# Second experts of an audio tower: the last 64 rows of the first product on half the array, slots in pairs

## What is computed

```
def _L1_ffn_ref(x, router_w, w1, w2):          # x = layernorm(h)
    logits = xt @ router_w.T ; probs = softmax(logits)
    topk_w, topk_idx = top_k(probs, 8) ; topk_w = topk_w / sum(topk_w)
    comb = zeros.at[token, topk_idx].add(topk_w)
    for e in range(16):
        h = gelu(xt @ w1[:, off:off + wd])
        out = out + comb[:, e:e + 1] * (h @ w2[off:off + wd, :])
```

## Time and profile before

| | before |
|---|---|
| three runs, median (lowest to highest) | 2683.68 us (2673.09 to 2688.26) |
| profiled execution, its own time | 2670.19 us |
| its span | 2668.2 us, mean granted clock 0.859 |
| TensorE busy (PE) over the span | 88% |
| VectorE, ScalarE, POOL busy | 68%, 58%, 3% |
| loads of d_1 and d_2 (3072 KB, 2304 KB), issue to landing | 11.6 and 16.6 us |

### The profile page before, as it was taken

The page is one execution under the profiler, slowest core; times in us unless marked ns, Lnnn a source line. Parts: engine busy times, 40 slices in busy tenths (PEclk is TensorE's granted clock), DMA queues, the critical chain, the costliest instruction groups (busy, mean ns, idle before and its releaser), DMA issues.

```text
span 2668.2 us, 40522 instructions
## 1 busy us (share of the span) xinstructions
PE 2355.6 (88%) x11650; PEld 2007.8 (75%) x11650; DVE 1826.5 (68%) x6297; ACT 1534.5 (58%) x4873; POOL 72.9 (3%) x46
## 2 busy tenths in 40 slices
PE   6778888999889998898988989878886999999999
PEld 2457667777768777777877877767775999899998
DVE  4278888989889898988989878887541322222223
ACT  2599887878768787776777766642111222222222
POOL 0000000000000000000000000000000101110110
PEclk7655587889889898888888879789986999999999
DMA  2000021222212221212222212223330000000000
GB/s 69 1 1 1 1 66 53 61 55 60 51 47 58 54 59 50 56 53 52 57 52 56 53 45 59 53 59 83 96 124 1 4 7 3 6 6 6 3 6 10
DMA packets 166682, 109.25 MB, mean 41 GB/s; under 512 B 15222, under 2 KB 165724, under 8 KB 166108
## 3 DMA queue, kind: packets, MB, share of 16 engines
q1 hardware_dynamic: 163872, 103.49, 14.5%
q10 hardware_dynamic: 2592, 3.33, 0.4%
HBM read 103.31 MB, written 3.20 MB: 40 GB/s over the span
## 4 chain that ended last, share of the span: by engine, by line
PE 44%; DVE 37%; issue 8%; ACT 6%; POOL 2%; another core or an unknown queue 1%; DVEq 1%; DMA 1%; SPq 0%; ACTq 0%; POOLq 0%
PE bank L503 20%; PE bank L848 7%; DVE late L1433 4%; DVE late L1295 3%; PE bank L617 3%; DVE late L1410 3%; DVE late L1407 3%; ACT late L972 3%; DVE late L1413 2%; DVE late L1403 2%; DVE late L1557 2%; PE bank L680 2%; POOL arena L485 2%; PE bank L582 2%; PE bank L738 2%
## 5 line engine op out<-in xcount | busy, mean ns | idle before, releaser
L972 ACT ACTIVATE late<-arena,late 125x250 bf16<-125x250 f32 x1152 | 565.0, 498 | 1.4 <-DVE late L1281 1.3
L1665 DVE TENSOR_TENSOR pair<-pair,arena 128x500 f32<-128x500 f32 x192 | 139.3, 726 | 444.8 <-PE bank L848 345.0
L503 PE MATMUL bank<-extra,wgu 128*128 128x250 f32 x1536 | 439.1, 437 | 0.0
L503 PE MATMUL bank<-xT,late 128*128 128x250 f32 x1536 | 360.6, 377 | 0.0
L503 PEld LDWEIGHTS bank<-extra,wgu 128*128 128x128 f32 x1536 | 326.7, 222 | 43.0 <-issue 2.2
L1138 ACT ACTIVATE pair<-bank 128x500 f32<-128x500 f32 x192 | 112.7, 587 | 382.9 <-PE bank L503 382.7
L503 PEld LDWEIGHTS bank<-xT,late 128*128 128x128 f32 x1536 | 286.5, 192 | 26.2
L617 PEld LDWEIGHTS bank<-vaug,late 125*125 125x125 f32 x1536 | 241.5, 233 | 76.0 <-ACT late L983 39.9
L848 PE MATMUL bank<-late,pair 128*125 128x192 f32 x1536 | 281.4, 326 | 0.0
L582 PE MATMUL bank<-late 16*125 16x251 f32 x768 | 251.8, 453 | 17.4 <-ACT arena L949 16.4
L848 PEld LDWEIGHTS bank<-late,pair 128*125 128x125 f32 x1536 | 259.3, 188 | 9.5 <-DVE pair L1665 0.2
(11 more groups left out here) (188 smaller groups left out, 3707.0 us busy)
## 6 DMA issues: line engine op xcount, KB each, us to landing
wgu<-in_b_g SPq DMA_DIRECT2D x192, 128.0 KB, 2.5
wgu<-in_b_u SPq DMA_DIRECT2D x192, 128.0 KB, 2.7
wdn<-in_b_d SPq DMA_DIRECT2D x192, 96.0 KB, 1.9
late<-comb_rows SPq DMA_DIRECT2D x128, 125.0 KB, 3.0
late<-comb_rows SPq DMA_DIRECT2D x128, 62.5 KB, 2.6
late<-in_d SPq DMA_DIRECT2D x1, 3072.0 KB, 11.6
out_h<-extra ACTq DMA_DIRECT2D x16, 187.5 KB
late<-in_d SPq DMA_DIRECT2D x1, 2304.0 KB, 16.6
```

The costliest lines, as they stand in the source:

```text
L503: ins = pe.matmul(dst, lhs(t), rhs(t), start=t == 0, stop=t == 1)
L972: ins = sc.activation(mk[:, n_par(u), t, :] if k == 3 else junk[:, t, :], s_sb[:, ub, t, 0:N], ACT.Sign, bias=thr[:, (n_par(u) + k + 1) % ...
L1665: dv.tensor_tensor(hid[:, s % 2, :, :], gl[:, s % 2, :, :], c, ALU.mult).then_inc(hid_set[1], 1)
```

## The change

In words: the product of channels 128 to 191 has 64 rows. The tiles are taken in pairs of slots (2j and 2j + 1). Slot 2j's 64-row weights lie on partitions 0 to 63, slot 2j + 1's on 64 to 127, and the products of the two slots go by turns to the lower and the upper half of the array: lower, upper, lower, upper. For the upper half the 64 channels must also lie on partitions 64 to 127 of `xT`, so VectorE writes them a second time into columns 192 to 255 of `xn`. The order on TensorE becomes first products 2j and 2j + 1, second products 2j - 2 and 2j - 1; the preparation of the next batch stands after pairs 0, 1 and 3. The first product's banks are four instead of three. The order on ScalarE, VectorE and POOL is the old one. The weights are loaded in three transfers.

```diff
         n_loads["c"] += 48
+        n_loads["d"] += 32
+        def m1_bank(s):
+            return bank[(1, 2, 3, 7)[s % 4]]
...
-                    sp.dma_start(w[name][:], d[name]).then_inc(loaded[k], 16)
+                    if name == "d_1":
+                        dst, of = w["d_1"], d["d_1"]
+                        sp.dma_start(dst[:, 0, :], of[:, 0, :]).then_inc(loaded[k], 16)
+                        for lo in (0, 1):
+                            half = dst[64 * lo:64 * lo + 64, 1, :].rearrange("p (t x n) -> p t x n", x=2, n=256)
+                            sp.dma_start(half[:, :, lo, :], of[0:64, 1, :].rearrange(
+                                "p (t x n) -> p t x n", x=2, n=256)[:, :, lo, :]).then_inc(loaded[k], 16)
+                    else:
+                        sp.dma_start(w[name][:], d[name]).then_inc(loaded[k], 16)
...
-            def m1_up(b, p, s):
-                ge(pe, gelu_set, 12 * b + s - 2)
-                for i in (0, 1):
-                    at = 128 * (2 * s + i)
-                    ins = two_k(bank[1 + s % 3][:, i * N:(i + 1) * N],
-                                lambda t: w["d_1"][:, t, at:at + 128], lambda t: xT[:, p, t, :])
-                ins.then_inc(up_ps[1], 1)
+            def m1_up(b, p, j):
+                ge(pe, gelu_set, 12 * b + 2 * j - 2)
+                X, Y = (m1_bank(2 * j + x) for x in (0, 1))
+
+                def product(U, x, i, k):
+                    tile = 4 * j + 2 * x + i
+                    lo = 0 if k == 0 else 64 * x
+                    hi = 128 if k == 0 else lo + 64
+                    return pe.matmul(U[:, i * N:(i + 1) * N], w["d_1"][lo:hi, k, 128 * tile:128 * tile + 128],
+                                     xT[lo:hi, p, k, :], start=k == 0 and i == 0, stop=k == 1,
+                                     skip_group_check=True)
+
+                for U, x in ((X, 0), (Y, 1)):
+                    for i in (0, 1):
+                        product(U, x, i, 0)
+                product(X, 0, 0, 1)
+                product(Y, 1, 0, 1)
+                product(X, 0, 1, 1).then_inc(up_ps[1], 1)
+                product(Y, 1, 1, 1).then_inc(up_ps[1], 1)
...
-                    for s in range(12):
-                        m1_up(b, p, s)
-                        if s >= 2:
-                            m1_down(b, p, s - 2)
-                        elif not first:
-                            m1_down(b - 1, 1 - p, 10 + s)
+                    for j in range(6):
+                        m1_up(b, p, j)
+                        for s in (2 * j - 2, 2 * j - 1):
+                            if s >= 0:
+                                m1_down(b, p, s)
+                            elif not first:
+                                m1_down(b - 1, 1 - p, 12 + s)
                         if not last:
-                            if s == 1:
+                            if j == 0:
                                 x_transpose(3, b + 1, 1 - p)
-                            if s == 2:
+                            if j == 1:
                                 route(1, b + 1, 1 - p)
-                            if s == 6:
+                            if j == 3:
                                 comb_transpose(1, b + 1, 1 - p)
...
+                    if ph == 3:
+                        ins = dv.tensor_scalar(xn[:, p, half, C:256], h[:, g, 128:C], mv[ph][:, g, 0:1],
+                                               rstd[ph][:, g, :], ALU.subtract, ALU.mult)
```

More of the change, by code:

```diff
@@ L1138, in body @@
                         sc.activation(gl[:, s % 2, :, :].rearrange("p i n -> p (i n)"),
-                                      bank[1 + s % 3][:, 0:2 * N],
+                                      m1_bank(s)[:, 0:2 * N],
                                       ACT.Gelu_apprx_tanh).then_inc(gelu_set, 1)
```

## The result

The changed kernel takes 2724.4 us in the median (2722.9 to 2728.1) against 2681.3 of the kernel before: a ratio of 1.0169 with a 95% interval of 1.0142 to 1.0196, 43 us slower. The changed kernel's profiled execution took 2728.1 us with a span of 2726.0. From the first broadcast to the end it is 664.9 us against 620.4, 44.5 more, and that is the change.

What follows compares the result with a forecast made beforehand. TensorE bounds the kernel now, but the change makes the chain from weights' transpose to input transposes the bound: 31.4 (ring) + 30 (clock) - 5.8 (four other batches) = +56 us on 2683.7, giving 2740 us, range 2703 to 2778.

Steps and rivals of the forecast that it cites:

- The ring: One second-expert batch, input transposes to weights' transpose and back through the fixed chain: 41.17 us against 38.55, twelve times.
- second leg: From the weights' transpose over ScalarE, POOL and VectorE to the next input transposes: 22.75 us, against 22.40 before.
- the 7.5 us: POOL's late start in the loop, behind the landing of ScalarE's row: taken as a fixed cost of some 7.5 us.
- The step for the first product: Eight 64-row records of a pair of slots take five spacings of 0.21 us, a gain of 0.63 us a pair.
- (b): Rival on the 64-row products: the halves overlap fully, four spacings, a pair of 5.53 us; 2727 us, chance 0.08.
- first leg: TensorE's stretch from the input transposes to the weights' transpose: 16.15 us before, 18.42 after, one more slot ahead.
- the four batches outside the ring: Batches where POOL starts early and TensorE stays late: six pairs each gain 0.24 us, 5.8 us in all.
- The clock: After TensorE's wait of 5.3 us the granted clock falls to 0.50 over 5 us: 2.5 us a batch, +30 us.
- The normalisation: Two more VectorE operations of 64 columns a batch, on the chain before the input transposes: 0.35 us for both.
- (a): Rival on the 64-row products: the halves don't run together, a pair takes 6.37 us; 2767 us, chance 0.20.
- (c): Rival on TensorE's granted clock: it holds behind the wait, the forecast without 30 us; 2710 us, chance 0.12.
- (d): Rival on POOL's start: tied to VectorE's weighting, so it comes sooner with pairs; 2667 us, chance 0.12.

Runs made afterwards that it cites:

- the filled wait: The changed kernel with 12 unneeded products ahead of the input transposes of batches 3 to 15, filling most of TensorE's wait: 2698.7 us.
- POOL written out: The changed kernel with POOL's 16 spreads written out instead of looped, so batch number and waits are constants: 2633.1 us.
- the fastest kernel: The changed kernel with POOL's spreads written out, weights' transpose before pair 3's second products, input transposes behind pair 1's first products: 2620.0 us.

## Why the prediction held, point by point

The forecast was 2740 us in a range of 2703 to 2778, slower with 0.81; measured were 2724.4, +43 instead of +56.

*The mechanism held.* The ring from the weights' transpose over ScalarE, the transfer, POOL and VectorE back to the input transposes is the bound of the changed kernel. Its second leg was put at 22.75 us and is 23.01 in the mean, counted between the same instructions (the 22.84 of the expectations starts 0.16 us later). That one place in the order is the price was shown by moving only it (2677.7), and that the chain is fixed on POOL's side by taking the 7.5 us out (2633.1).

*The step for the first product was mis-sized.* I took five spacings for eight records, because the two records of one product follow each other; four is right, the size of rival (b). A pair is 5.53 us, not 5.74. The first leg at the full clock is 17.78 us where 18.42 was taken, 0.64 a batch less, 7.7 in all, and the four batches outside the ring gained 7.8 us instead of 5.8. The Trainium skill, TensorE: Matmul & The Clock Gate, section "Part 3: Packing small matmuls", has products in strict program order; taken record by record that would have given five spacings, and the traces don't agree with it here. The "up to 2x" that the prediction takes from the Trainium skill, TensorEngine Tiling (Array Packing), stands there in the section "Theoretical Speedup", not in "The Solution"; the traces agree with it for the 64-row products. That going to part of the rows and back costs 0.2 us each holds: the loads of 64 rows start 0.32 us behind the end of those before them, twice a pair, and 5.98 - 4 x 0.21 + 0.39 = 5.53.

*The clock was mis-sized.* I took 2.5 us a batch; the fall costs 2.12. The waits of 5.1 to 6.3 us brought it in all twelve batches, as foreseen, but the low clock ended some 4 us behind the wait (at 2315.0, the wait ending at 2311.0) and not 5: 4.6 us less in all. Against these stand 0.26 us a batch of the second leg, 3.1 us more. The terms close: 7.7 + 4.6 + 2.0 - 3.1 = 11.2 us under the forecast of 55.6, that is 44.4, where the traces have 44.5 from the first broadcast on and the medians 43.

*The normalisation.* L1226 and L1229 take 1.17 us from the first start to the transposes (2309.84 to 2311.01), against 0.72 before: 0.45 where 0.35 was taken. The rest of the 0.26 lies between POOL's small addition and its broadcast, whose starts are 6.45 us apart in the mean instead of 6.06, less 0.2 us by which the addition starts sooner behind the sending. In nine of the twelve batches the addition itself takes 0.34 to 0.73 us instead of 0.18.

*Rivals.* (b), given 0.08, is what happened as far as the halves go. Its 2727 us came nearer than the forecast, but partly by luck: it took the clock 0.4 us a batch too high, the gain of the four outer batches 3 us too high and the second leg 0.26 us a batch too low, which nearly cancel. (a) and (c) fall with the runs on one half and with the filled wait. (d), the faster side, put POOL's start down to VectorE as the profile did: the starts stay 10 us behind the sending in the pair order, and fall to 2.2 us with the same semaphores. What I had called a fixed cost was fixed only by where the step back stands in POOL's program; that it could be moved I had not asked.

*What I left out.* That VectorE's weighting of slot 0 needs second product 10, which by itself makes a wait of 0.5 us in the new order, is in none of my steps. In the changed kernel the longer wait covers it in the loop; outside the loop it cost most of the 3 us by which the four batches gained less than six faster pairs. The wait of the kernel before, put at 1.2 us, is 0.91 in the mean of its twelve (10.9 in all), so TensorE was to stand 5.0 us, not 5.3; it stood 5.1 to 6.3.

## What to carry to other kernels

A faster product is worth what the chain around it leaves: before an engine's work is cut or reordered, follow its waits back to where they close a ring with the engine itself, and count how many of its instructions lie in each leg. An edit that moves one small instruction of that ring by a slot can cost more than the faster products bring, and moving it earlier cost nothing here. Where a wait is put down to an engine that had long been done, look at what the waiting engine does between its wait and its next instruction; here one throwaway operation in POOL's idle time was worth some 90 us.

## What the runs showed of the hardware

Eight 64-row records in 32-bit, by turns on the lower and upper half, take 1.05 us (0.21 of it for the change from 128 rows to 64), and 1.88 on one half; the two records of one product do not hold up the other half. Changing between 128 rows and part of them costs 0.2 us each way for 16 rows and for 64.

POOL's step from an ordinary operation to its broadcast takes 5.85 us, and the step back 6.7 to 7.7 us in the run with the added operation. The Trainium skill, GPSIMD Engine Reference, section "2.1 Instruction dispatch", has some 6 us for the first call of a newly loaded routine; the traces agree for the way to the broadcast, and the way back is dearer.

While the broadcast runs, VectorE's weighting stands: two of them take 4.19 us together instead of 1.3 (the changed kernel with POOL written out, 2305.09), and 2.23 in the fastest kernel. The Trainium skill, SBUF — State Buffer, section "Terms", has VectorE and GpSimd share a port pair that one of them holds for a whole instruction, and the traces agree. What it costs TensorE, if anything, none of the runs takes apart.
